# Attention in pairs of key tiles, pair sums on GpSimd, reciprocals by logarithm and exponential, one mask product for several heads

## What is computed

```python
h = _layernorm(x) * (1 + ca) + sa
q = rmsnorm(apply_rope((h @ Wq.T) per head))       # 16 heads of 32
k = rmsnorm(apply_rope(h @ Wk.T)); v = h @ Wv.T    # one head of 32
scores = einsum('bhqd,bkd->bhqk', q, k) * scale    # causal mask
attn = softmax(scores)
out = einsum('bhqk,bkd->bhqd', attn, v)
out = rmsnorm(out, w_pre) @ Wo.T
x = x + ga * out
x = x + gb * ffn(_layernorm(x) * (1 + cb) + sb)    # routed experts and a shared one
```

## Time and profile before

| | |
|---|---|
| median of 3 runs | 1417.44 us (1413.54 to 1420.72) |
| profiled execution, its own time | 1412.17 us |
| its span | 1410.3 us |
| TensorE busy | 1202.0 us (85%) |
| VectorE busy | 1045.8 us (74%) |
| ScalarE busy | 697.0 us (49%) |
| GpSimd busy | 623.1 us (44%) |

### The profile page before, as it was taken

The page is one execution under the profiler, slowest core; times in us unless marked ns, Lnnn a source line. Parts: engine busy times, 40 slices in busy tenths (PEclk is TensorE's granted clock), DMA queues, the critical chain, the costliest instruction groups (busy, mean ns, idle before and its releaser), DMA issues.

```text
span 1410.3 us, 25182 instructions
## 1 busy us (share of the span) xinstructions
PE 1202.0 (85%) x8680; PEld 881.0 (62%) x8680; DVE 1045.8 (74%) x1962; ACT 697.0 (49%) x1399; POOL 623.1 (44%) x496
## 2 busy tenths in 40 slices
PE   3697888989998886999996289999999999999960
PEld 3434555545555453554443178999999999999950
DVE  3456877777665788777652546889999999999978
ACT  0223334344554332343551033678787778777730
POOL 0201211111045412362137045478788787877841
PEclk9888899999999888799997589999999999999985
DMA  8107100000000000000000256699999999999987
GB/s 310 75 1 258 73 1 16 1 9 9 2 14 7 8 9 12 9 1 9 9 13 16 70 92 125 190 299 298 298 301 297 304 290 302 298 299 300 292 219 253
DMA packets 80465, 189.94 MB, mean 135 GB/s; under 512 B 15538, under 2 KB 15922, under 8 KB 80130
## 3 DMA queue, kind: packets, MB, share of 16 engines
q1 hardware_dynamic: 43828, 110.30, 23.7%
q0 software_dynamic: 32800, 71.46, 21.6%
q10 hardware_dynamic: 3760, 7.17, 1.3%
HBM read 136.31 MB, written 52.64 MB: 134 GB/s over the span
## 4 chain that ended last, share of the span: by engine, by line
PE 60%; DVE 15%; issue 6%; DMA 5%; POOL 4%; DVEq 4%; ACT 4%; ACTq 0%; POOLq 0%; SPq 0%
PE ps L1027 15%; PE ps L1051 9%; PE ps L892 8%; PE ps L854 5%; PE ps L879 4%; PE ps L915 4%; PE ps L825 4%; DVE nmax L1220 3%; PE ps L1011 3%; POOL slot_dram L472 3%; DMA acc_dram<-y,slots 3%; PE ps L868 2%; PE ps L817 1%; DMA rw<-in_router_t 1%; ACT probs L644 1%
## 5 line engine op out<-in xcount | busy, mean ns | idle before, releaser
L1220 DVE TENSOR_REDUCE nmax<-ps 128x1 f32<-128x512 f32 (+3 forms) x352 | 195.8, 587 | 136.6 <-PE ps L857 78.3
L644 ACT ACTIVATE probs<-ps 128x512 f32<-128x512 f32 (+1 forms) x320 | 160.2, 554 | 272.5 <-PE ps L879 271.9
L551 POOL DMA_INDIRECT acc_dram<-y,slots x128 | 249.3, 1948 | 80.7 <-issue 48.9
L854 PE MATMUL ps<-kpad,qpT 128*128 128x512 f32 (+3 forms) x384 | 166.0, 492 | 63.5 <-DVE nmax L1220 39.3
L496 POOL TENSOR_SCALAR_AFFINE_SELECT probs<-probs 128x512 f32<-128x512 f32 x64 | 43.4, 678 | 347.6 <-ACT probs L644 347.5
L472 POOL DMA_INDIRECT slot_dram<-pay,idx x128 | 129.4, 1011 | 83.3 <-issue 47.8
L854 PEld LDWEIGHTS ps<-kpad,qpT 128*128 128x128 f32 x384 | 76.5, 211 | 131.5 <-DVE nmax L1220 73.6
L536 POOL DMA_INDIRECT xg<-h_dram,slots x128 | 129.7, 1013 | 49.7 <-issue 30.8
L879 PE MATMUL ps<-qT,kT 98*128 98x512 f32 (+1 forms) x320 | 118.1, 448 | 3.0 <-ACT qT L633 1.7
L1027 PE MATMUL ps<-x_hi,e_gu_hi 128*112 128x256 f32 (+1 forms) x768 | 120.1, 278 | 0.0
L1027 PE MATMUL ps<-x_hi,e_gu_lo 128*112 128x256 f32 (+1 forms) x768 | 119.6, 278 | 0.0
(11 more groups left out here) (210 smaller groups left out, 2456.7 us busy)
## 6 DMA issues: line engine op xcount, KB each, us to landing
e_gu<-in_gate_up SPq DMA_DIRECT2D x64, 704.0 KB, 7.5
e_d<-in_w_down SPq DMA_DIRECT2D x64, 224.0 KB, 4.6
acc_dram<-h SPq DMA_DIRECT2D x2, 4608.0 KB, 26.0
e_d<-in_w_down SPq DMA_DIRECT2D x64, 128.0 KB, 5.4
xres<-in_x SPq DMA_DIRECT2D x4, 1024.0 KB, 11.7
wmod_b<-in_wmod SPq DMA_DIRECT2D x2, 2048.0 KB, 14.6
h_dram<-h SPq DMA_DIRECT2D x16, 256.0 KB, 2.0
xg<-h_dram SPq DMA_DIRECT2D x16, 256.0 KB, 5.9
```

Source lines behind the costliest of these rows:

```text
L551: pool.indirect_dma_start(out=acc_dram[a], out_offset=bass.IndirectOffsetOnAxis(ap=slots[:, at:at + 1], axis=0), in_=y[e % 2][:, h, :], in ...
L644: act.activation(probs[:, n % PROBS, 2 * pr:2 * pr + 2, off:CW], unit_bank(2 * n + pr)[:, :, off:CW], ACT.Exp).then_inc(s_exp, 1)
L854: last = pe.matmul(view[:, a, :], qpT[:, t % 2, (first + a) // GH, :], kpad[:, (first + a) % GH, lo:hi], start=True, stop=not diagonal)
L1220: dve.tensor_reduce(nmax[:, 1 if lo else 0, first:first + heads], max_view(n, heads, hi - lo), AX.X, ALU.max, negate=True).then_inc(s_max, 1)
```

## The change

Steps are taken in pairs of key tiles. `values(q, g, k)` runs in the place of the odd step's `values`, with both tiles' products by `v_sb`; for all pairs but a group's last, GpSimd adds the two tiles' exponentials (`add_pair`, one 128 x 1024 addition into the single buffer `both`), and TensorE multiplies the sum by `ones` when it takes the next pair. `PROBS` becomes 4. The last, diagonal pair is still multiplied by `ones` tile by tile. `copy_out` takes the logarithm of the sums and, behind the semaphore that frees the bank, the exponential of its negative, from one function table that is loaded ahead of the loop; `divide` is a single product. `pieces_at` puts as many heads into a bank as fit in 512 columns, and one bf16 product adds the bias to all of them. `normalise` and the second high part of the queries (`second_high`) move from VectorE to ScalarE; `qh`, `kh4` and `qr` are gone, and so are the second buffers of `xn` and `hT`; `shift` has two operations in place of three. The first layer norm's centre is multiplied once on GpSimd.

```diff
-PROBS = 3
+PROBS = 4
 LAG = 2
+LN_EXP_SET = 6
...
+        def heads_in(width):
+
+            return min(GH, 512 // width)
+
         def pieces(i):
 
-            return H // 2 if i < 2 else H if i < 4 else 2 * H
+            width = (i + 1) * P
+            if width <= 512:
+                return H // heads_in(width)
+            return H + H // heads_in(width - 512)
 
         def pieces_before(t):
 
             return sum(pieces(k % TPB) for k in range(t))
 
         def pieces_at(i, h):
-
-            if i < 2:
-                return [(h // 2, h, 2, 0, (i + 1) * P)] if h % 2 == 0 else []
-            if i < 4:
-                return [(h, h, 1, 0, (i + 1) * P)]
-            return [(2 * h, h, 1, 0, 512), (2 * h + 1, h, 1, 512, (i + 1) * P)]
+            width = (i + 1) * P
+            if width <= 512:
+                k = heads_in(width)
+                return [(h // k, h, k, 0, width)] if h % k == 0 else []
+            k = heads_in(width - 512)
+            found = [(h + h // k, h, 1, 0, 512)]
+            if h % k == k - 1:
+                found.append((h + h // k + 1, h + 1 - k, k, 512, width))
+            return found
...
+        def pairs_added(q, g, k):
+
+            before = sum(NG * (keys(c) // 2 - 1) for c in range(q)) + g * (keys(q) // 2 - 1)
+            return before + min(k, keys(q) // 2 - 1)
+
+        def pairs_freed(n):
+
+            for q in range(NCHUNK):
+                for g in range(NG):
+                    for k in range(keys(q) // 2):
+                        if step_of(q, g, 2 * k) == (n - PROBS) // 2 * 2:
+                            return pairs_added(q, g, k + 1)
...
+            def add_pair(q, g, k):
+                n = step_of(q, g, 2 * k)
+                pool.wait_ge(s_exp, 2 * n + 4)
+                if pairs_added(q, g, k):
+                    pool.wait_ge(s_bsum, pairs_added(q, g, k))
+                pool.tensor_tensor(both[:, :, :], probs[:, n % PROBS, :, :], probs[:, (n + 1) % PROBS, :, :], ALU.add)\
+                    .then_inc(s_both, 1)
...
+                    for q, g, kt in steps_at(t * H + h, 1):
+                        if kt % 2 and kt < keys(q) - CT:
+                            add_pair(q, g, kt // 2)
...
+            def normalise(t):
+                if t % TPB == 0:
+                    act.wait_ge(s_rstd, t // TPB + 1)
+                if t:
+                    act.wait_ge(s_xT, t)
+                act.activation(xn[:, :], xtile(t), ACT.Identity, bias=center[:, t:t + 1], scale=rstd[:, t:t + 1])\
+                   .then_inc(s_xn, 1)
+
+            def second_high(t):
+                act.wait_ge(s_t2, t + 1)
+                if t >= 2:
+                    act.wait_ge(s_st, (t - 1) * NG)
+                act.activation(qs[:, t % 2, :, HD:2 * HD].bitcast(f32r), t2[:, 0:H, :], ACT.Copy).then_inc(s_hi2, 1)
...
-                    act.wait_ge(s_pv, n - PROBS + 1)
+                    act.wait_ge(s_pv, (n - PROBS) // 2 + 1)
+                    if pairs_freed(n):
+                        act.wait_ge(s_both, pairs_freed(n))
...
-                act.wait_ge(s_pv, step_of(q, g, keys(q) - 1) + 1)
+                act.wait_ge(s_pv, step_of(q, g, keys(q) - 1) // 2 + 1)
...
-                act.activation(oT[:, q % 2, g, :], ps[:, PV_BANK, 0:CW], ACT.Copy)
-                act.activation(sums_s[:, g % 2, :], ps[:, PV_BANK, CW:2 * CW], ACT.Copy).then_inc(s_on, 1)
+                total = sums_s[:, g % 2, :]
+                act.activation(total, ps[:, PV_BANK, CW:2 * CW], ACT.Ln)
+                act.activation(oT[:, q % 2, g, :], ps[:, PV_BANK, 0:CW], ACT.Copy).then_inc(s_on, 1)
+                act.wait_ge(s_on, q * NG + g + 1)
+                act.activation(total, total, ACT.Exp, scale=-1.0).then_inc(s_rec, 1)
...
+            act.add_instruction(mybir.InstLoadActFuncSet(name=nc.get_next_instruction_name(), act_func_set_id=LN_EXP_SET))
...
+                    if h == 7 and 0 <= t + 3 < NT:
+                        normalise(t + 3)
+                    if h == 9 and 0 <= t + 1 < NT:
+                        second_high(t + 1)
...
-                pe.transpose(ps[:, X_BANK, P:2 * P], kh4[:, :, :].rearrange("p j d -> p (j d)"), ident)
                 for g in range(NG):
                     last = pe.transpose(ps[:, Y_BANK, g * P:(g + 1) * P],
-                                        qh[:, GH * g:GH * g + GH, :].rearrange("p j d -> p (j d)"), ident)
+                                        t2[:, GH * g:GH * g + GH, :].rearrange("p j d -> p (j d)"), ident)
...
-                    view = max_view(n, heads, hi - lo)
+                    view, diagonal = max_view(n, heads, hi - lo), hi == (i + 1) * P
                     for a in range(heads):
-                        diagonal = hi == (i + 1) * P
                         last = pe.matmul(view[:, a, :], qpT[:, t % 2, (first + a) // GH, :],
-                                         kpad[:, (first + a) % GH, lo:hi], start=True, stop=not diagonal)
-                        if diagonal:
-                            last = pe.matmul(view[:, a, hi - lo - P:hi - lo], ident_b[:, :], bias_b[:, :], start=False,
-                                             stop=True)
+                                         kpad[:, (first + a) % GH, lo:hi], start=(a == 0),
+                                         stop=(a == heads - 1 and not diagonal))
+                    if diagonal:
+                        last = pe.matmul(view[:, :, hi - lo - P:hi - lo], ident_b[:, :],
+                                         bias_b[:, :].unsqueeze(1).to_broadcast([P, heads, P]), start=False, stop=True)
...
-            def values(q, g, kt):
-                b, off, n = q // CPB, first_query(q, kt), step_of(q, g, kt)
-                if kt == 0 and q * NG + g:
+            def values(q, g, k):
+                b, n, last_pair = q // CPB, step_of(q, g, 2 * k), keys(q) // 2 - 1
+                if k == 0 and q * NG + g:
                     pe.wait_ge(s_on, q * NG + g)
-                if kt >= keys(q) - CT:
-                    pe.wait_ge(s_mask, masks_before(q, g, kt) + 1)
+                if k == last_pair:
+                    pe.wait_ge(s_mask, masks_before(q, g, 2 * k + 1) + 1)
                 else:
-                    pe.wait_ge(s_exp, 2 * n + 2)
-                for left, at in ((v_sb[:, b, kt, :], 0), (ones[:, :], CW)):
+                    pe.wait_ge(s_exp, 2 * n + 4)
+                for kt in (2 * k, 2 * k + 1):
+                    off = first_query(q, kt)
                     for j in range(GH):
-                        last = pe.matmul(ps[HD * j:HD * j + HD, PV_BANK, at + off:at + CW], left,
-                                         probs[:, n % PROBS, j, off:CW], start=(kt == 0 and at == 0),
-                                         stop=(kt == keys(q) - 1 and at == CW))
-                last.then_inc(s_pv, 1)
+                        last = pe.matmul(ps[HD * j:HD * j + HD, PV_BANK, off:CW], v_sb[:, b, kt, :],
+                                         probs[:, (n + kt % 2) % PROBS, j, off:CW], start=(kt == 0), stop=False)
+                if k:
+                    pe.wait_ge(s_both, pairs_added(q, g, k))
+                    for j in range(GH):
+                        last = pe.matmul(ps[HD * j:HD * j + HD, PV_BANK, CW:2 * CW], ones[:, :], both[:, j, :],
+                                         start=False, stop=False)
+                    last.then_inc(s_bsum, 1)
+                if k == last_pair:
+                    for kt in (2 * k, 2 * k + 1):
+                        off = first_query(q, kt)
+                        for j in range(GH):
+                            last = pe.matmul(ps[HD * j:HD * j + HD, PV_BANK, CW + off:2 * CW], ones[:, :],
+                                             probs[:, (n + kt % 2) % PROBS, j, off:CW], start=False, stop=(kt % 2 == 1))
+                if k == 0 or k == last_pair:
+                    last.then_inc(s_pv, 1)
+                else:
+                    pe.sem_inc(s_pv, 1)
...
-                        values(q, g, kt)
+                        if kt % 2:
+                            values(q, g, kt // 2)
...
-                    dve.tensor_copy(q_parts[:, :, HD:2 * HD].bitcast(f32r), t2[:, 0:H, :])
...
-                    dve.tensor_copy(qh[:, :, :].bitcast(f32r), t2[:, 0:H, :])
                     dve.tensor_copy(ks[:, 0:HD].bitcast(f32r), t1[:, H, :])
                     dve.tensor_copy(ks[:, 2 * HD:3 * HD].bitcast(f32r), t1[:, H, :])
-                    dve.tensor_copy(kh4[:, :, :].bitcast(f32r), t1[:, H, :].unsqueeze(1).to_broadcast([P, GH, HD]))
...
-            def divide(q, g, n):
-                total = sums_s[:, g % 2, :]
-                if n == 0:
-                    dve.wait_ge(s_on, q * NG + g + 1)
-                if n < CT:
-                    piece = total[:, n * P:(n + 1) * P]
-                    dve.reciprocal(piece, piece)
-                else:
-                    dve.drain()
```

(10 more changed lines are left out.)

53 lines of the change are left out of this document (25 added, 28 removed).

## The result

The changed kernel takes 1440.5 us (median of 4 runs, 1437.14 to 1443.1) against 1415.49 us before (4 runs, same chip): a ratio of 1.0183, 95% interval 1.0122 to 1.0244. Run again on another chip it gave 1.0124 (1.0071 to 1.0177). It is slower, by some 22 us. The prediction said 1387 us, 2.1% faster, and gave the times above 1424 us 8 in 100. The profiled execution has a span of 1435.3 us (1410.3 before).

A forecast was written before the change was run, and what follows sets the result against it. TensorE has most of the attention stage's chain, and it and VectorE feed each other through two banks, neither full. Terms -24 - 12 + 3 + 5 + 4 - 3 = -27 on 1412.2 us gave 1385, as median 1387 us; range 1358 to 1410.

The forecast's parts named there:

- the pairs' products: TensorE: summing a pair first saves one step's products by ones, 0.5 us; 12 us in q = 3 and 7, 8 outside.
- the loop: q = 3 and 7: GpSimd's addition, ScalarE's exponentials and TensorE's products wait in a 5.7 us circle; 20 us of new waiting.
- VectorE's relief: Attention stage: 97 us of reciprocals, casts, normalising, shift and reductions leave VectorE; a quarter comes back, 24 us.
- TensorE's share outside the pairs: Outside q = 3 and 7: fewer bias products, 3 us, and `kh4`'s packing transpose, within a 12 us term that includes pairs' 8.
- ScalarE's additions: Attention stage: moved normalising, copies and exponentials add 30 us of ScalarE work, of which a tenth costs 3 us.
- the clock: TensorE's clock in windows with waits was 0.84 to 0.94; a tenth of the cost, 3 us, is given back.
- the addition's length: GpSimd: one 128 x 1024 addition takes 2.6 us, bounds 1.36 and 4.1.
- the group's change: q = 3 and 7: the next group's first values come a slot later than before, no longer waiting for `copy_out`; saves 3 us.
- The shared port: Chunks outside q = 3 and 7: each of 24 GpSimd additions can hold back one VectorE operation; 4 us, bounds 0 and 31.
- rival 2: Additions meet VectorE's work in q = 1, 2, 5, 6 nearly each time: 31 us, 1414; chance 0.13, shared with 4 us additions.
- the loop doesn't close: Groups with six key tiles: two slots and a third of a slot lie between, over 2 us each, so no waiting there.
- the longer q = 7: Sign: chunk q = 7 takes longer than 66.4 us; otherwise the addition is short or the loop isn't closed.

The follow-up runs named there:

- Idle additions: 48 GpSimd additions of constants that nobody waits for, added to the kernel without pairs (0.9925, again 0.9911) and to the one in pairs without additions (1.0031).
- idle powers: 48 GpSimd powers of 12 columns that nobody reads, added to the kernel without pairs at the places of the idle additions: 0.9735.

## Why the prediction was wrong

The way from before to after, in ratios turned into us (each step some 5 to 8 us uncertain):

| step | from, to | us |
|---|---|---|
| the change without its pairs | 1, 0.972 | -39 |
| values in pairs | 0.972, 0.990 | +24 |
| 48 additions that nobody waits for | 0.990, 1.003 | +19 |
| 192 products by ones fewer, and waiting for the additions, two buffers | 1.003, 0.999 | -5 |
| one buffer in place of two | 0.999, 1.015 | +23 |
| sum | 1, 1.015 | +22 |

The forecast's sum was -27 and the result is +22, 49 us apart. The order of the values accounts for 24 of them, the pairs' products and the loop together for 21 (-3 forecast, +18 measured), and the hold on VectorE for 15. The rest of the change gave 11 more than forecast, which goes the other way.

**Right in kind, low in size: what the rest of the change gives.** VectorE's relief, TensorE's share outside the pairs, ScalarE's additions and the clock were priced at -24, -4 (bias products and `kh4`), +3 and -3: -28 without the pairs' products, for a measured -39. Without additions VectorE's busy time falls from 1045.8 to 959.4 us, 86 of the 97 predicted, and ScalarE's rises from 697.0 to 727.7, by 30.7 of 30. The reciprocals gave 18 us, a third of their work where a quarter was taken.

**Right: the addition's length.** 2.40 us for 2.6. The Trainium skill (GPSIMD Engine Reference, Performance versus the Vector engine) led to an estimate of 2.25 us; the trace has 2.40.

**Right in kind, in part by luck: the loop.** Its waiting was put at 20 us and the single buffer costs 23. The length of 5.7 us, which was taken for two intervals in each group, holds for the second of them: 5.6 us in q = 7 and 5.6 to 6.3 in q = 3. The first has 7.8 to 9.3 us in q = 7 and 8.5 to 11.9 in q = 3, so the total agrees better than what it was added from.

**Wrong: what the pairs' products save.** The forecast set 12 us of products and 3 us for the group's change against the loop, and 8 more us of products outside it: 23 us in all. With two buffers the saved products and the waits for the additions come to -5 together. The waits are part of it: `causal` behind an addition was priced at nothing, since the next scores would cover it, and it ended 9.6 us of TensorE's idle time, 4.38 of them at the end of the stage, where no scores follow. How the rest divides was not measured.

**Wrong: "The shared port", 4 us.** It cost 19 us in pairs and 27 by step. The prediction had the mechanism, and three things in its size were wrong. It counted 24 additions, as if only those outside q = 3 and 7 met VectorE. Compared record by record with the median of its form in the kernel without pairs, from 100 to 770 us, 61 VectorE instructions on SBUF alone (on the kernel's own tiles, without PSUM) overlap an addition, and 27 of them are longer, the 61 by 37 us together; 12 of the 27 lie in q = 3 and 7. The 47 that read PSUM are not longer at all. It then took half, for which it gave no row; its rival 2 says that VectorE's time is mostly reductions out of PSUM. But what counts is whether one instruction on SBUF comes up within 2.4 us, and one is enough to hold the queue until the addition ends. And it took a quarter of the hold as lying on the path, by VectorE's share of the chain: by step, VectorE is busy 41 us more and the kernel takes 27 us more, two thirds; in pairs it is 19 of 45 us. A hold is not like work taken out evenly. The one above stops `nmax<-nmax`, which joins the two halves of a tile's maxima, and the next chunk's scores need these. The Trainium skill (SBUF — State Buffer, Who interferes with whom) has the rule: a VectorE instruction with two SBUF inputs, or in a 2-port mode, and a GpSimd instruction that reads SBUF block each other for a whole instruction. The trace agrees for the additions (0.17 us become 2.17), while a power of 12 columns, 2.3 us long and reading SBUF too, holds nobody. Rival 2 named this cost, 31 us, and gave it too little weight.

**Wrong, and the largest: the order of the values had no price.** The sum has terms for the pair's additions and products, none for the fact that two steps' scores now follow each other directly through two banks. This was 24 us, as much as the loop. The rows were there: in the earlier trace rows the values stand between two scores, start with the exponentials and cover them (0.46 + 0.54 us for 1.08 of ScalarE). Taking them out of there exposes the exponentials once a pair, as the timeline in pairs shows; the 24 us themselves were measured as a whole.

**Borne out: "the loop doesn't close" with six key tiles.** Of the 33.5 us that ScalarE waits for an addition, 30.6 lie in q = 3 and 7, and 3.0, in two waits, elsewhere. Halving the addition gave back 34 us, of which 15 intervals of 1.1 us explain 16. The hold on VectorE falls from 37 to 11 us by the same count; at the 19 of 45 found above that is another 11. The other 7 are as large as the uncertainty.

**The clock** was to give back 3 us. It is 0.906 over the changed kernel's profiled execution and 0.930 without pairs, and in q = 7, where TensorE now stands, 0.90 for 1.00. So the clock took time instead of giving it back, and part of each cost above is the clock's. How much wasn't separated.

Of the prediction's signs, the longer q = 7, the length of the addition and ScalarE's 30 us came. Chunks q = 1 and 5 were to be 5 to 8 us shorter and are 3.4 shorter and 1.5 longer, and VectorE is busy 50 us less in place of 97.

What stays open: the costs were measured along one path, and they overlap. Idle additions cost 19 us in pairs, where idle powers weren't run beside them, and 27 by step, and the products that the pairs save are worth 5 us in pairs and 14 by step (0.9918, the mean of two, to 0.9820). The loop's 23 us rests on the mean of two measurements of the changed kernel, 18 and 27 us taken one by one.

## What to carry to other kernels

Before work is regrouped, look in the timeline at what now stands between two instructions that share a buffer: values between two scores hid ScalarE's exponentials here, and taking them away cost more than the products they saved. Work moved to an idle engine isn't free because the engine is idle: count the instructions of its neighbour that work on SBUF alone and come up while it runs, and price each at what is left of the long instruction; VectorE's share of the chain gave too little here. When one edit of several is slow, measure the others without it: here they were worth 39 us.
